# Closing operations of an iteration set singly among the next one's big operations, harmonics loaded an iteration ahead, dense input rows, search rows of 500

## The reference, cut to what matters

```python
x = silu(edge_radial @ W1 + b1); x = silu(x @ W2 + b2); tpw = x @ W3 + b3
hs_e = hs[src]; hv_e = hv[src]
m0 = ALPHA * (einsum('eu,euw->ew', hs_e * sh0[:, None], W00)
              + INV_SQRT3 * einsum('eui,ei,euw->ew', hv_e, sh1, W110))
m1 = ALPHA * (einsum('eu,ei,euw->ewi', hs_e, sh1, W01)
              + einsum('eui,euw->ewi', hv_e * sh0[:, None, None], W10))
agg = segment_sum(concatenate([m0, m1.reshape(-1, 24)]), dst) / sqrt(16)
...
x = layernorm(x + h_self + agg)
e = leaky(s_src[src] + s_dst[dst]); alpha = softmax of e over the edges of one dst
x = layernorm(x + segment_sum(x[src] * alpha, dst))
```

## Time and profile before

| | us |
|---|---|
| median of 3 runs | 7802.65 (7799.65 to 7808.03) |
| the profiled execution | 7802.29 |
| its span in the profile | 7800.5 |
| first layer's loop | about 71 to 4231 |
| block loop of the second layer | about 4460 to the end |
| busy: GpSimd, TensorE, VectorE, ScalarE | 5841.8, 5624.8, 5018.7, 3438.8 |

### The profile page before, as it was taken

How to read it: one execution, slowest core, us unless ns; L and a number is a source line. 1 busy time by engine, 2 the same in 40 slices (tenths; PEclk the granted TensorE clock), 3 DMA queues, 4 the chain that set the end, 5 groups by cost and what they waited for, 6 DMA issues and landing times.

```text
span 7800.5 us, 80145 instructions
## 1 busy us (share of the span) xinstructions
PE 5624.8 (72%) x21671; PEld 3136.9 (40%) x21671; DVE 5018.7 (64%) x8628; ACT 3438.8 (44%) x4929; POOL 5841.8 (75%) x6031
## 2 busy tenths in 40 slices
PE   5666666666666666677676168888888888888881
PEld 3444444444444444444444034444444444444440
DVE  6888888888888888888886344444444444444442
ACT  3444444444444444433332145555555555555550
POOL 6777777777777777777775777777777777777776
PEclk7777777777777777777776589999999999999995
DMA  3111111111111111111112022222222222222221
GB/s 90 36 36 36 36 36 36 36 36 36 36 36 36 36 36 36 36 37 35 35 37 42 18 46 45 42 45 45 45 45 41 45 45 45 45 43 44 45 45 24
DMA packets 317381, 313.15 MB, mean 40 GB/s; under 512 B 165444, under 2 KB 261604, under 8 KB 316690
## 3 DMA queue, kind: packets, MB, share of 16 engines
q0 software_dynamic: 192800, 129.34, 14.2%
q1 hardware_dynamic: 124562, 183.61, 7.1%
HBM read 201.63 MB, written 110.86 MB: 40 GB/s over the span
## 4 chain that ended last, share of the span: by engine, by line
POOL 54%; issue 27%; DMA 6%; DVE 4%; ACT 4%; PE 3%; SPq 1%; POOLq 0%; DVEq 0%; ACTq 0%
POOL early L396 25%; POOL prod L396 24%; DMA idx<-in_src 3%; PE tpw L539 3%; POOL msgs L396 3%; DMA early<-in_x_wide,idx 2%; ACT sums L611 2%; DVE red L817 1%; POOL starts L400 1%; DVE red L819 1%; POOL dst_row L396 1%; ACT early L691 1%; DVE msgs L855 1%; PE hid L539 0%; ACT hv L571 0%
## 5 line engine op out<-in xcount | busy, mean ns | idle before, releaser
L396 POOL DMA_INDIRECT early<-in_x_wide,idx x3126 | 3078.6, 985 | 1001.1 <-issue 961.6
L396 POOL DMA_INDIRECT prod<-table,idx x2500 | 2369.1, 948 | 761.9 <-issue 757.9
L539 PE MATMUL tpw<-xs,early 128*128 128x462 bf16 x7000 | 2043.3, 375 | 516.2 <-ACT early L691 389.4
L495 PE MATMUL tpw<-w3s,early 128*128 128x256 f32 x6252 | 1853.3, 458 | 154.1 <-DVE prod L805 153.8
L495 PEld LDWEIGHTS tpw<-w3s,early 128*128 128x128 f32 x6252 | 1396.7, 231 | 749.8 <-DVE prod L805 296.6
L488 PE MATMUL hid<-hid,w2s 128*128 128x384 f32 x1044 | 541.8, 607 | 1062.1 <-ACT hid L558 1062.1
L539 PE MATMUL tpw<-big,early 128*128 128x462 bf16 x3500 | 1300.6, 372 | 0.0
L539 PEld LDWEIGHTS tpw<-xs,early 128*128 128x128 bf16 x7000 | 687.8, 100 | 1303.4 <-issue 610.4
L564 ACT ACTIVATE early<-hid,b2s 64x384 f32<-64x384 f32 x1044 | 598.0, 573 | 886.3 <-PE hid L484 879.8
L683 ACT ACTIVATE early<-early,bases 128x640 f32<-128x640 f32 x875 | 710.6, 827 | 21.4 <-issue 0.2
L817 DVE TENSOR_REDUCE red<-prod 128x144 f32<-128x1152 f32 x521 | 703.2, 1350 | 15.8 <-DMA starts<-msgs 11.4
(11 more groups left out here) (170 smaller groups left out, 5666.7 us busy)
## 6 DMA issues: line engine op xcount, KB each, us to landing
scan<-prod SPq DMA_DIRECT2D x125, 425.0 KB, 2.5
early<-in_x_wide,idx POOLq DMA_INDIRECT x3126
scan<-sums SPq DMA_DIRECT2D x130, 384.0 KB, 2.8
early<-qrows SPq DMA_DIRECT2D x126, 320.0 KB, 4.5
prod<-table,idx POOLq DMA_INDIRECT x2500
early<-in_radial_t SPq DMA_DIRECT2D x262, 48.0 KB
big<-in_sh SPq DMA_DIRECT2D x1, 5904.0 KB, 34.3
idx<-in_src SPq DMA_DIRECT2D x262, 6.0 KB, 1.7
```

Source lines behind the costliest of these rows:

```text
L396: return pool.indirect_dma_start(out=dest, out_offset=None, in_=source, in_offset=bass.IndirectOffsetOnAxis(ap=index, axis=0))
L495: mm = pe.matmul(tpw_v(b)[:, t, :], hid2[:, b, at:at + P], w3s[:, :], start=True, stop=True)
L539: mm = pe.matmul(found[i][:, 0:BC], hot[k][:, g, i * P:(i + 1) * P], split(s, g), start=g == 0 and s == 0, stop=g == NBATCH - 1 and s == S ...
```

## The change

`messages` is split into its eleven operations, and these, `carry_in` and the four scans become the 16 steps of `finish`. `groups` puts four steps of the iteration behind into each slot: one behind the first big product, one behind the second (and behind `bprod`, where the slot has one), one behind the first reduction, one behind the second. `red` gets a second buffer, in the tile `early`. The slot numbers (`find_slots`) are computed in slot 1 of the first iteration. The harmonics come 96 columns at a time, each iteration's in the `refill` of the one before; `bsum` waits for them. FIRSTS is 800, so a search row has 500 entries. `x` is loaded as 32 dense columns a node, at the end of `xs`, and after the last `refill`; `qrows` is stored after the first `refill`.

```diff
-FIRSTS = 3200
+FIRSTS = 800
 ROW = E // FIRSTS
...
-OPENING = 8 * 4 * CT
+SHC = 4 * CT
...
-        xs = xs_f[:, 0:NJ * TW].rearrange("p (j w) -> p j w", w=TW)[:, :, 0:D]
+        xs = xs_f[:, NJ * (TW - D):NJ * TW].rearrange("p (j d) -> p j d", d=D)
...
-        red = sb("red", [P, NC, MUL, CT])
+        red = [sb("red", [P, NC, MUL, CT]), early_red]
...
-            sp.dma_start(big[:, 0:OPENING], sh[:, 0:OPENING]).then_inc(sh_in, 16)
+            sp.dma_start(big[:, 0:SHC], sh[:, 0:SHC]).then_inc(sh_in, 16)
...
-            sp.dma_start(big[:, OPENING:], sh[:, OPENING:]).then_inc(sh_rest_in, 16)
...
             def refill(it):
+                sp.wait_ge(sh_in, it * 16 + 16)
+                sp.dma_start(big[:, bass.ds(it * SHC + SHC, SHC)],
+                             sh[:, bass.ds(it * SHC + SHC, SHC)]).then_inc(sh_in, 16)
                 for h in range(2):
...
+            refill(0)
             sp.wait_ge(qrows_ready, 1)
             sp.dma_start(qrows, row_q).then_inc(qrows_out, 16)
-            refill(0)
...
+            refill(ITERS - 1)
             sp.wait_ge(row_counted, SEARCHES)
             sp.dma_start(xs[0:P, :, :], x.rearrange("(p j) d -> p j d", p=P)).then_inc(x_in, 16)
-            refill(ITERS - 1)
...
                 dve.wait_ge(hv_ready, n + 1)
+                dve.wait_ge(sh_in, it * 16 + 16)
...
+            def finish(it, m, tiles, step):
+
+                if step < 3:
+                    by_sh1(it, m, tiles, step)
+                elif step < 7:
+                    by_sh0(it, m, tiles, step - 1)
+                elif step < 11:
+                    message(it, m, tiles, step - 7)
+                elif step == 11:
+                    carry_in(it, m, tiles)
+                else:
+                    scan(it, m, step - 12, tiles)
...
-                    products(g, k, k % 2, it * 2 + h)
+                    product_a(g, k, k % 2, it * 2 + h)
+                    if behind is not None:
+                        finish(behind, 1 - m, CT, 4 * k)
+                    product_b(k, k % 2)
                     if k == 0 and behind is None:
                         find_starts()
+                    if k == 1 and behind is None:
+                        find_slots()
...
-                    if k == 0 and behind is not None:
-                        carry_in(behind, 1 - m, CT)
-                    red_k = reduce(g, k)
+                    if behind is not None:
+                        finish(behind, 1 - m, CT, 4 * k + 1)
+                    reduce_a(g, k, m)
+                    if behind is not None:
+                        finish(behind, 1 - m, CT, 4 * k + 2)
...
-                    if behind is not None:
-                        scan(behind, 1 - m, k, CT)
+                    red_k = reduce_b(k, m)
                     if k == SLOTS - 1:
                         red_k.then_inc(red_ready, 1)
-                        messages(it, m, CT)
+                    if behind is not None:
+                        finish(behind, 1 - m, CT, 4 * k + 3)
```

More of the change, by code:

```diff
@@ L116, in build @@
         xs_f = sb("xs", [P, max(NJ * TW, FIRSTS)])
-        xs = xs_f[:, 0:NJ * TW].rearrange("p (j w) -> p j w", w=TW)[:, :, 0:D]
+        xs = xs_f[:, NJ * (TW - D):NJ * TW].rearrange("p (j d) -> p j d", d=D)
+        assert all((b + 1) * BC <= NJ * (TW - D) + (b + 1) * BJ * D for b in range(NBATCH))
         result = xs_f[:, 0:NJ * D].rearrange("p (j d) -> p j d", d=D)
@@ L169, in build @@
         firsts = xs_f[:, 0:FIRSTS].bitcast(I32)
[L170 removed]
+        junk_at = rows_end + 2 * BLOCKS * PT + PC
+        junk = early[:, junk_at:junk_at + FIRSTS // 2].bitcast(BF16)
         nodes_s = sb("nodes_s", [P, SEARCHES + 1])
@@ L759, in _, with find_slots @@
             dve.tensor_scalar(w110, w110, 1.0 / 3.0 ** 0.5, None, ALU.mult).then_inc(w3_scaled, 1)
-            dve.wait_ge(pe_edges_in, 32)
-            link(slot(src_pe_i.bitcast(I32), amod[:, :], rounded[:, :]))
-            link(dve.scalar_tensor_tensor(out=amod[:, :], in0=rounded[:, :], scalar=-float(BJ), in1=amod[:, :],
-                                          op0=ALU.mult, op1=ALU.add))
-            slot(row_i32.bitcast(I32), rounded_row, row_q).then_inc(qrows_ready, 1)
+            def find_slots():
+                dve.wait_ge(pe_edges_in, 32)
+                link(slot(src_pe_i.bitcast(I32), amod[:, :], rounded[:, :]))
+                link(dve.scalar_tensor_tensor(out=amod[:, :], in0=rounded[:, :], scalar=-float(BJ), in1=amod[:, :],
+                                              op0=ALU.mult, op1=ALU.add))
+                slot(row_i32.bitcast(I32), rounded_row, row_q).then_inc(qrows_ready, 1)
             def find_starts():
@@ L792, in bsum_end, with product_a @@
                    .then_inc(b_ready, 1)
-            def products(g, k, b, n):
+            def product_a(g, k, b, n):
                 w = tpw_v(b)
@@ L803, in products, with product_b @@
                     rows[:, k, :, 0:3 * MUL].unsqueeze(2).to_broadcast([P, GT, MUL, 3 * MUL]), ALU.mult)
+            def product_b(k, b):
+                w = tpw_v(b)
                 tiles = slice(k % HALF * GT, (k % HALF + 1) * GT)
@@ L820, in reduce @@
                                          prod_b[k % 2].rearrange("p (t i u) -> p t i u", t=GT, u=MUL), AX, ALU.add)
-            def messages(it, m, tiles):
-                sh_c = sh_v[:, bass.ds(it, 1), :, 0:tiles].rearrange("p o k t -> p (o k) t")
-                sh0 = sh_c[:, 0:1, :].to_broadcast([P, MUL, tiles])
-                dve.wait_ge(red_ready, it + 1)
-                for i in range(3):
-                    dve.tensor_tensor(tmp[:, i, :, 0:tiles], red[:, 1, :, 0:tiles],
-                                      sh_c[:, 1 + i:2 + i, :].to_broadcast([P, MUL, tiles]), ALU.mult)
-                for j in range(2, NC):
-                    ins = dve.tensor_tensor(red[:, j, :, 0:tiles], red[:, j, :, 0:tiles], sh0, ALU.mult)
-                ins.then_inc(scaled, 1)
-                dve.wait_ge(scaled, it + 1)
-                out = msgs(m, tiles).rearrange("p (j w) t -> p j w t", j=4)
-                for i in range(3):
-                    dve.tensor_tensor(out[:, 1 + i, :, :], tmp[:, i, :, 0:tiles], red[:, 3 + i, :, 0:tiles], ALU.add)
-                dve.tensor_tensor(out[:, 0, :, :], red[:, 0, :, 0:tiles], red[:, 2, :, 0:tiles],
-                                  ALU.add).then_inc(msgs_ready, 1)
@@ new lines, in by_sh, with by_sh1, by_sh0 @@
+            def by_sh(it, tiles):
+                return sh_v[:, bass.ds(it, 1), :, 0:tiles].rearrange("p o k t -> p (o k) t")
+            def by_sh1(it, m, tiles, i):
+                if i == 0:
+                    dve.wait_ge(red_ready, it + 1)
+                dve.tensor_tensor(tmp[:, i, :, 0:tiles], red[m][:, 1, :, 0:tiles],
+                                  by_sh(it, tiles)[:, 1 + i:2 + i, :].to_broadcast([P, MUL, tiles]), ALU.mult)
+            def by_sh0(it, m, tiles, j):
+                ins = dve.tensor_tensor(red[m][:, j, :, 0:tiles], red[m][:, j, :, 0:tiles],
+                                        by_sh(it, tiles)[:, 0:1, :].to_broadcast([P, MUL, tiles]), ALU.mult)
+                if j == NC - 1:
+                    ins.then_inc(scaled, 1)
@@ new lines, in message @@
+            def message(it, m, tiles, j):
+                out = msgs(m, tiles).rearrange("p (j w) t -> p j w t", j=4)
+                if j == 0:
+                    dve.wait_ge(scaled, it + 1)
+                    dve.tensor_tensor(out[:, 0, :, :], red[m][:, 0, :, 0:tiles], red[m][:, 2, :, 0:tiles], ALU.add)
+                else:
+                    ins = dve.tensor_tensor(out[:, j, :, :], tmp[:, j - 1, :, 0:tiles], red[m][:, 2 + j, :, 0:tiles],
+                                            ALU.add)
+                    if j == 3:
+                        ins.then_inc(msgs_ready, 1)
@@ L890, in _ @@
             groups(ITERS - 1, 1, ITERS - 2, 1)
-            products(LAST, 0, 0, 2 * ITERS)
-            carry_in(ITERS - 1, 1, CT)
-            for part in range(D // PIECE):
-                scan(ITERS - 1, 1, part, CT)
-            reduce(LAST, 0).then_inc(red_ready, 1)
+            product_a(LAST, 0, 0, 2 * ITERS)
+            product_b(0, 0)
+            for step in range(16):
+                finish(ITERS - 1, 1, CT, step)
+            reduce_a(LAST, 0, 0)
+            reduce_b(0, 0).then_inc(red_ready, 1)
             dve.wait_ge(sums_ready, ITERS - 1)
-            messages(ITERS, 0, REST)
-            carry_in(ITERS, 0, REST)
-            for part in range(D // PIECE):
-                scan(ITERS, 0, part, REST)
+            for step in range(16):
+                finish(ITERS, 0, REST, step)
             dve.wait_ge(scanned, ITERS + 2)
```

20 lines of the change are left out of this document (10 added, 10 removed).

## The result

The changed kernel takes 7705.89 us (median of 4 runs, 7705.23 to 7707.49) beside 7802.57 of the kernel before (4 runs, 7799.65 to 7808.03). The ratio is 0.9875 with a 95% interval of 0.9863 to 0.9888. The forecast was 7698 in a range of 7650 to 7770. The profiled execution's span is 7703.4 us, for 7800.5 before: 97.1 us less.

The account below looks back on a forecast made before the run. The prediction took GpSimd's gathers to pace the first layer, with 126 us lost to VectorE's two-SBUF-input operations in flight at their starts. Gains 69 + 27 + 8 = 104 from 7802.3 gave 7698 us, range 7650 to 7770.

Parts of the forecast that it names:

- (1): First layer's loop: closing operations one by one cut gather delays from 126 to 57 us, gain 69 us (12 to 126).
- the walk: First layer's loop: closing operations placed in the gathers' cycle from `bprod` on; four cross a gather's start, 0.44 us an iteration.
- (2): First layer's loop: harmonics loaded an iteration ahead, one more DMA and an already met wait before `bprod`; cost 0.
- (3): First layer: search rows of 500 and 800 firsts; the `dst` gather moves 2000 instead of 500 bytes a partition; cost 0.
- (4): Start: fewer bytes ahead of `idx` and `qrows` after the refill; GpSimd resumes at 44 for 71, gain 27 us.
- (5): First layer's end: `x` after the refill in one piece a partition, less 2.6 us of longer tail; gain 8 us.
- the stretch: Rival, loop: long gathers stay, as by the skill's rule or a cause of their own; only (4) and (5), 7767 us; chance 0.08.
- hardly a single meets a gather: Rival, loop: single closing operations hold almost no gather; 126 + 35 = 161 us go, 7641 us; chance 0.08.
- held gathers got in without a gap in VectorE's queue: Denies the slower rival, loop: a held gather enters only at a gap in VectorE's queue; 8350 us, chance 0.07.

Follow-up runs that it names:

- e3: Kernel before with the closing burst's eleven operations replaced by one-input reductions of the same sizes (harmonics' products and sums left out); 7691.97 us for 7789.41.
- e10: Changed kernel with the two waits ahead of `bprod` swapped, so the one for `hv` stands last; 7682.72 us, ratio 0.9909 to the kernel before.
- e0: The changed kernel run once more, unedited, on another chip; 7692.11 us, ratio 0.9921 to the kernel before on that chip.
- e7: Changed kernel with `qrows` (127 rows) stored ahead of the first `refill`, on the chip with the slow kernel before; 10393.91 us for 10236.47.
- e2: Changed kernel with the closing burst put back behind the last reduction, `carry_in` and scans at their old places, new loads kept; 7794.41 us, ratio 1.001 to the kernel before.
- e8: Changed kernel with 128 rows instead of 127 in `src_rows` and `qrows`, on the chip with the slow kernel before; 10362.72 us, ratio 1.0123 to the kernel before.

## Why the prediction was right, point by point

- **What bounds the kernel**: GpSimd's queue, with VectorE's second SBUF input as the cause of the long gathers. Right, and e3 shows it: 97 us less with one input in the burst, and no gather over 1.5 us, where the trace of the kernel before has 110.
- **(1), 69 us**: 61 us measured. The mechanism was right, the walk mis-sized: meetings of 57 us forecast, 66.3 measured (0.51 us an iteration for 0.44). I took `bprod` at its old place in the cycle, 0.57 us, and the wait for `sh_in` moved it by 0.1 us (e10: 10 us of delays); the cost of that added wait I had put at 0. In this trace `bprod` begins at 0.68 (median) in the half with the scans, so the scan behind it begins near 1.06 instead of 0.95 and stands 0.20 us old when the next gather starts, as at 1009.76. That one meeting made 21 us, 0.17 an iteration, where I had 0.06. The other meetings of that half sum to 0.26 us for the 0.27 of the walk, those of the other half to 0.08 for 0.11.
- **Luck in (1)**: the 126 us that I took off were those of one trace on one chip. On the chip of e0 the same change gave 57.4 us, little over half of the forecast 104, since the kernel before, by the estimate above, has less to lose there. Nothing in the prediction allowed for that.
- **(2), 0**: the harmonics are never late, but see the wait above. (3), 0: GpSimd's gather of a `dst` row of 2000 bytes takes 0.946 us by mean for 0.943. Right.
- **(4), 27 us**: 30.2 measured, resuming at 39.86 for 44, and the wait of about 1 us for `prod` came at 55.76. The bytes ahead of `idx` were given most of the weight; e7 shows that with these bytes gone the place of `qrows` can still cost all 31 us. How the gain parts between the two isn't measured.
- **(5), 8 us**: 8.4.
- **What the profile would show**: no gather above 1.4 us (longest 1.255), 3.7 an iteration above 0.96, mean 0.966, VectorE's wait for `hv` 588.7 us in 128 iterations, 4.6 each, for 4.3 forecast. The block loop unchanged. "Issue" wasn't the only releaser named, but the gaps put down to `idx` and `prod` are 0.30 us long like the rest.
- **Rivals**: the stretch went, "hardly a single meets a gather" was off by the 66 us of meetings, and held gathers got in without a gap in VectorE's queue. None of them considered that the pace could be TensorE's; on a chip where it is, the sum doesn't hold at all.

## What to carry to other kernels

Where GpSimd's indirect gathers set the pace, what another engine has in flight at a gather's start is the thing to look at, not the totals: sort by that moment, make operations of one input where possible, and keep two-input ones short and between starts. A change that only shifts phases can give or take as much as the change that was meant, as e2 did; read the delays in the trace and not the time alone. For the same reason the size of such a gain belongs to the chip it was measured on: 97 us on one, 57 on another. And a gain on the pacing engine holds only while that engine sets the pace, which can differ from chip to chip.

## What the runs showed of the hardware that was not expected

- A memset of 0.78 us with a two-input product directly behind it holds a gather that starts in the memset to the end of both (up to 0.95 us, all 256 cases); memsets of 0.20 to 0.37 us ahead of operations with one input, or one from PSUM, held none of 310.
- A cast of 3125 int32 elements holds as well: in e8 the gather of 40.91 went on at 41.61, 0.12 us before the cast (39.95, 1.78 us) ended, and in the changed kernel the gather of 33.06 took 2.16 us beside the same cast. The gather of 42.85 in e8 took 3.15 us beside one two-input operation of 3.41 us.
- A second semaphore wait, long met, behind the one that ends last delayed the next instruction of VectorE by 0.09 us.
- The kernel before took 7749 to 7803 us on three chips and 10236 on another, with a granted clock of TensorE of 0.74 there; in e8 on that chip a gather still takes 0.944 us, and TensorE stands idle 1744 us in the block loop for nothing that the profile shows.
